# The state's part of the attention numerators as four 32-column products, the second state sum ahead of them, and the state layouts earlier on VectorE

## What is computed

```python
qkv = x @ wqkv                                   # 256 -> 768, 16 heads of 16 channels
q, k = relu(q), relu(k)
kv  = cumsum(k[..., :, None] * v[..., None, :], axis=2)
num = einsum('bhnd,bhnde->bhne', q, kv)
den = einsum('bhnd,bhnd->bhn', q, cumsum(k, axis=2))[..., None] + 1e-5
attention = (num / den).reshape(b, n, d) @ wo

scores = sigmoid(x @ Wr)                         # router, 8 experts, the best 2 are taken
hid = silu(x @ Wg[e]) * (x @ Wu[e])              # 4 experts with a hidden width of 128
ffn = sum_e cw[e] * (hid[e] @ Wd[e]) + (cw[4] + cw[6]) * x + cw[7] * relu(x) + conv4(x) + conv_b
```

## Time and profile before

| | before |
|---|---|
| median of 3 runs | 1421.67 us (1413.32 to 1422.32) |
| the profiled execution's own time | 1417.17 us |
| its span, first to last instruction | 1415.4 us |
| granted TensorE clock, mean | 0.994 of full speed |
| TensorE matmuls (PE) busy | 1373.6 us, 97% |
| TensorE weight loads (PEld) busy | 1194.5 us, 84% |
| VectorE (DVE) busy | 1087.9 us, 77% |
| GpSimd (POOL) busy | 811.6 us, 57% |
| ScalarE (ACT) busy | 734.5 us, 52% |

### The profile page before, as it was taken

One profiled execution on the slowest core, in us unless ns is written; L12 is line 12 of the kernel. 1 busy time (PEld: TensorE's weight loads), 2 busy tenths in 40 slices (PEclk: granted clock), 3 DMA queues, 4 the chain that ended last, 5 costly groups with the idle time before them and its releaser, 6 DMA issues.

```text
span 1415.4 us, 55195 instructions
## 1 busy us (share of the span) xinstructions
PE 1373.6 (97%) x23392; PEld 1194.5 (84%) x23392; DVE 1087.9 (77%) x2566; ACT 734.5 (52%) x1545; POOL 811.6 (57%) x679
## 2 busy tenths in 40 slices
PE   4999999999999999999999999999999999999997
PEld 3788887888888888888888888888888888878886
DVE  5778787778787778877777877788877788867874
ACT  5455554455554455554555554455544555535551
POOL 1755665655656655656556657556556556565553
PEclk9899999999999999999999999999999999999998
DMA  5011101111111121011111011111111111101110
GB/s 168 4 63 62 62 33 33 62 62 62 47 48 32 62 62 63 32 38 56 62 63 59 35 38 56 63 62 47 47 32 63 62 62 43 51 32 47 47 47 16
DMA packets 46790, 73.86 MB, mean 52 GB/s; under 512 B 6480, under 2 KB 42192, under 8 KB 42448
## 3 DMA queue, kind: packets, MB, share of 16 engines
q1 hardware_dynamic: 46544, 70.24, 14.7%
HBM read 53.18 MB, written 17.04 MB: 50 GB/s over the span
## 4 chain that ended last, share of the span: by engine, by line
PE 95%; DVE 2%; issue 1%; SPq 1%; ACT 1%; DMA 0%; DVEq 0%; ACTq 0%
PE ring L311 48%; PE scores L311 16%; PE ring L432 9%; PE ring L422 6%; PE scores L368 5%; PE state_sum L383 4%; PE scores L321 2%; PE ring L450 2%; PE scores L350 2%; DVE sm L764 1%; DMA x_t<-in_L_attn_x_dram 0%; DVE x_t L836 0%; SPq L268 0%; DVE cT L786 0%; ACT qp L527 0%
## 5 line engine op out<-in xcount | busy, mean ns | idle before, releaser
L637 POOL TENSOR_TENSOR hid<-hid,cwb 128x512 f32<-128x512 f32 x128 | 163.1, 1275 | 217.4 <-DVE hid L794 214.6
L786 DVE SCALAR_TENSOR_TENSOR cT<-xT,conv_ws,cT 128x512 f32<-128x512 f32 x192 | 256.9, 1377 | 0.0
L625 POOL TENSOR_TENSOR x_t<-x_t,same 128x1024 f32<-128x1024 f32 x32 | 76.9, 2404 | 286.3 <-ACT same L534 286.3
L550 ACT ACTIVATE sg<-ring 128x512 f32<-128x512 f32 x128 | 76.7, 599 | 303.1 <-PE ring L311 303.1
L311 PE MATMUL ring<-xl,wgu_h 128*128 128x512 f32 x512 | 212.9, 416 | 8.7 <-DVE x_t L836 6.8
L311 PE MATMUL ring<-xh,wgu_l 128*128 128x512 f32 x512 | 203.5, 397 | 0.0
L311 PE MATMUL ring<-xh,wgu_h 128*128 128x512 f32 x512 | 202.6, 396 | 0.0
L490 ACT ACTIVATE yh<-yT 128x256 fp32r<-128x256 f32 x128 | 53.6, 418 | 286.7 <-DVE yT L807 286.7
L794 DVE TENSOR_TENSOR hid<-ring,sg 128x512 f32<-128x512 f32 x128 | 88.2, 689 | 137.4 <-PE ring L311 137.2
L641 POOL TENSOR_TENSOR hl<-hid,hh 128x512 fp32r<-128x512 f32 x128 | 193.0, 1508 | 0.0
L764 DVE TENSOR_TENSOR sm<-scores,causal_s 128x512 f32<-128x512 f32 x256 | 159.0, 684 | 29.1 <-PE scores L368 28.6
(11 more groups left out here) (110 smaller groups left out, 3591.1 us busy)
## 6 DMA issues: line engine op xcount, KB each, us to landing
cwb<-cw_rows SPq DMA_DIRECT2D x32, 1024.0 KB, 4.8
x_t<-in_L_attn_x_dram SPq DMA_DIRECT2D x32, 512.0 KB, 5.2
out_dram<-x_t SPq DMA_DIRECT2D x32, 512.0 KB, 3.0
cw_rows<-cwt SPq DMA_DIRECT2D x128, 2.0 KB, 1.4
sm<-in_L_attn_wqkv_dram SPq DMA_DIRECT2D x2, 384.0 KB, 4.9
sm<-in_L_ffn_Wg_dram SPq DMA_DIRECT2D x2, 256.0 KB, 4.7
sm<-in_L_ffn_Wu_dram SPq DMA_DIRECT2D x2, 256.0 KB, 5.4
cwb<-in_L_ffn_Wd_dram SPq DMA_DIRECT2D x1, 512.0 KB, 5.6
```

The lines of the kernel that those rows point to most:

```text
L550: act.activation(sg[:, :], GB[t % 2], ACT.Silu).then_inc(s_sg, 1)
L625: pool.tensor_tensor(xb, xb, same[:, :, :], ALU.add).then_inc(s_base1, 1)
L637: pool.tensor_tensor(hid[:, e, :], hid[:, e, :], cwb[:, e, :], ALU.mult).then_inc(s_hid, 1)
L786: ins = dve.scalar_tensor_tensor(out=cT[:, c, :], in0=xT[:, j % 2, c, n:n + BT], scalar=conv_ws[:, c, n:n + 1], in1=cT[:, c, :], op0=ALU.m ...
```

## The change

The products with the state are cut by columns: in place of one matmul with 128 stationary columns there are four (m = 0 to 3) with 32 columns each, which write 32 partitions of the result each. All four read the same 64 columns of q on all 128 rows. The wait on s_bd for both chunks of the tile stands once, ahead of them. `state_sum(2t + 2)` moves from behind these products to ahead of them, right behind the products within the chunks. On VectorE `blocks(2t + 2)` moves ahead of `gate_up(t)` and `blocks(2t + 3)` ahead of the wait on s_num; before, both stood in `attend`, the second behind the product into `yT`.

```diff
@@ numerators (TensorE)
+                    if t < T - 1:
+                        state_sum(s, j, 0, 2 * t + 2)
+                    pe.wait_ge(s_bd, chunk_at(s, j, 2 * t + 1))
                     for h in range(2):
                         if first_tile and h == 0:
                             continue
-                        n = 2 * t + h
-                        pe.wait_ge(s_bd, chunk_at(s, j, n))
+                        n0 = t * P + h * HALF
                         for g in range(C):
-                            n0 = t * P + h * HALF
-                            ins = mm(NB2[t % 2][h][:, g * HALF:(g + 1) * HALF], state_bd[:, n % 4, g * P:(g + 1) * P],
-                                     qT[:, g, n0:n0 + HALF], start=False, stop=True, skip_group_check=True)
+                            for m in range(PPG):
+                                cols = slice(g * P + BLK * m, g * P + BLK * m + BLK)
+                                ins = mm(NB2[t % 2][h][BLK * m:BLK * m + BLK, g * HALF:(g + 1) * HALF],
+                                         state_bd[:, (2 * t + h) % 4, cols], qT[:, g, n0:n0 + HALF], start=False,
+                                         stop=True, skip_group_check=True)
                     ins.then_inc(s_num, 1)
-                    if t < T - 1:
-                        state_sum(s, j, 0, 2 * t + 2)
@@ attend and the loop over tiles (VectorE)
                 def attend(t):
-                    if t < T - 1:
-                        blocks(s, j, 0, 2 * t + 2)
-                    elif j < BPS - 1:
-                        blocks(s, j, 1, 0)
                     dve.wait_ge(s_num, at(s, j, T, t + 1))
...
+                for t in range(T):
+                    if t < T - 1:
+                        blocks(s, j, 0, 2 * t + 2)
+                    elif j < BPS - 1:
+                        blocks(s, j, 1, 0)
+                    gate_up(t)
                     if t < T - 1:
                         blocks(s, j, 0, 2 * t + 3)
-
-                for t in range(T):
-                    gate_up(t)
                     attend(t)
```

## The result

The changed kernel takes 1504.53 us in the median of 4 runs (1494.96 to 1506.51), the kernel before 1418.29 us (4 runs): 1.060 times as long, 95% interval 1.053 to 1.066. Faster was forecast; it is slower by 6%.

What follows compares the result with a forecast made beforehand. TensorE's sequence was taken as the bound. Savings of 37.8 us (88 full tiles), 1.9 (8 first tiles) and 7.4 (32 tiles t = 3), together 47 us from 1417.2, gave 1370, named 1371 us; range 1344 to 1398 us.

Steps and rivals of the forecast that it cites:

- What bounds the kernel: TensorE's own sequence, busy 97% of the span; time taken out counts in full while VectorE keeps up.
- The price p: Distance between starts of the new 128-row, 32-column records at line 435: 0.017 us, low end 0.010, high end 0.029.
- the two rivals with a higher price: Weight loads one at a time, 0.029 us, 1416 us (9%); column tiles on same rows not overlapping, 0.031 us, 1615 us (6%).
- the second of them: Line 435: column tiles on the same rows don't overlap, each record pays its tile's whole turn; 198 us lost, 1615 us (6%).
- The stretch of a tile: TensorE from the last record of line 422 to `gate_up`: 1.44 us before, 0.94 after, plus 0.07 for the wait.
- The wait of the second sum: `state_sum(2t + 2)` at line 383 waits for `blocks(2t + 2)` to read the bank it overwrites: 0.07 us a tile.
- the saved switch: Shape switch from line 432 to 383, up to 0.22 us; moved, the sum follows line 422 in the same shape at 0.02.
- VectorE: Keeps up, level with TensorE in t = 3; the rival that `blocks(2t + 2)` starts late gives 1396 us (12%).
- No transfer and no other queue is moved: Statement that the change leaves transfers and other queues alone; no term of the sum stands for them.

Runs made afterwards that it cites:

- e1_order: The changed kernel with the four old 128-column products per tile, so only the new order of sums and layouts: 1410.68 us against 1420.56, ratio 0.994.
- g1_cols64_pad40: The changed kernel with two 64-column products in place of four 32-column ones, and 40 tiny matmuls ahead of the loop: 1379.02 us against 1421.05, ratio 0.971.
- g2_cols64_pad44: The changed kernel with two 64-column products in place of four 32-column ones, and 44 tiny matmuls ahead of the loop: 1402.76 us, ratio 0.988.

## Why the prediction was wrong

**What bounds the kernel** held: TensorE's own sequence set the time before, and sets it now.

**The price p** was near: 0.017 us was taken and 0.014 measured, though no trace had shown the shape. Tiles over all 128 rows overlap, and the two rivals with a higher price (0.029 us, and over 0.031) fall with it. The kernel did end slower, as the second of them had it, but not by its mechanism. The two rules of the Trainium skill that stood beside those rivals, the floor of about 25 ns between starts and loads that overlap only where the row group differs, find no support in the 0.014 us.

**The stretch of a tile** came out at 1.05 us, where 0.94 and 0.07 for the wait were forecast. The wait of the second sum was mis-sized: line 383 starts 0.20 us behind the last record of line 422 in that tile, so it waits some 0.18 us; over the tiles without a stall it starts 0.09 to 0.20 us behind. The lower p makes up for it, and the stretch to `gate_up` is 0.96 to 1.04 us in the 16 such tiles. The order's own worth, which the sum has at 0.22 for the saved switch less 0.02 and 0.07, in 96 tiles 12 us, is 10 us in `e1_order`.

**VectorE** kept up: in `g1_cols64_pad40`, 42 us faster than before, it is 81% busy and no wait of TensorE for `state_bd` shows.

**The step that failed** is the one without a term. The prediction counts the added records, 24 in a full tile, at what they cost in the array, and says "No transfer and no other queue is moved". But TensorE's instructions are themselves a transfer: 24 more packets of 16.4 KB, and, what matters, 128 records in a row from line 383 to line 435, started within about 1.7 us (746.61 to 747.84 for the first 96, and 0.43 for line 435 where it isn't stopped). Where the grid cuts the program so that such a row fills a block, the block runs in 1.6 to 2.4 us, and the next one takes longer to come: its packet starts 0.8 to 1.4 us behind the block's start, takes about 1.0 us, and the engine goes on some 1.4 us behind its end, 3.5 us in all by the middle values. A late block cost 0.7 to 2.6 us from start to start, one or two blocks behind it came late too, and the idle time took the clock to half in places. 36 us of work were saved; 99 us of idle time and 26 us of clock were lost. The 64-column form at a lucky address comes within 8 us of the forecast of 1371 us: 1379 us. The 32-column form that was forecast was never seen without stalls.

The trace of the kernel before had a hint. Four of its issue waits lie in the last sequence, which stands behind the loop at other places of the grid. Three are at records 20764, 20890 and 21015, 126 and 125 apart, the first behind a block of 2.3 us; the fourth is at 21522, behind 125 records in 2.8 us. All four end 1.2 to 1.4 us behind a packet of the instruction queue. I took the 1% "issue" of the chain as nothing to explain.

**What stays open.** The packets' times answer in part why blocks behind a late one are late too, although they ran for 4.4 to 7.2 us. In the changed kernel, where one late block follows another, the packet starts only 3.8 to 6.8 us behind the restart, when the block that runs has nearly ended, in place of 0.8 to 1.4 us; a series ends where it comes early again (1.1 us behind the restart at record 1954). Why it starts late is not shown. The block of 2.2 to 2.4 us that ends at record 951 and brings no stall has no packet in it: in the sequence read, the packet ahead of it had started 2.8 us before the block began (642.74 against 645.5 us), so the next block was there. And in `g2_cols64_pad44` the block of 3.8 us had its packet only 2.0 us behind its start. So the bound isn't the block's length alone but when its packet starts, and what sets that start is open. That the block is late because it is being fetched is read from the grid, the shifts and the packets' ends; the profile itself names no releaser.

## What to carry to other kernels

Count instructions, not only array time: where a change splits a matmul into short ones, look at how long some 125 load-and-matmul records in a row take, and expect stalls of about 2 us, and in places the half clock behind them, where that is under 3 to 4 us. Stalls that name no releaser, fall between two records of one line and come back at the same record of each iteration are such stalls; a few tiny matmuls ahead of the loop move them, and are the cheapest test. The instruction queue's packets in the trace are the other one: here the stalls ended about 1.4 us behind one. And a kernel's time, before or after a change, can hang on such a shift by 6% (1419 us with 5 tiny matmuls, 1511 us with 27), so a change that adds or removes TensorE instructions should be judged at more than one.

## What the runs showed of the hardware

- Four column tiles over all 128 rows overlap: 32-column float32 records that move 64 columns start 0.014 us apart; two 64-column tiles need (0.69 - 0.23) / 15 = 0.031 us a record, so the same work in half the records takes nearly the same time (0.46 against 0.43 us).
- The waits for instructions are mostly 0.9 to 2.6 us from start to start and stand at fixed records, on a grid of 256 instructions or 124 to 126 records; each ended 1.2 to 1.9 us behind a packet of the instruction queue. A loop's jump cost 1.6 to 3.0 us in every kernel, and ended 1.5 to 1.7 us behind such a packet.
- Behind the idle stretch from 748.2 to 750.2 us the granted clock was 0.50 until 753.6; such falls came 20 times in the changed kernel and 4 times before, over the span 34.6 us of lost clock against 8.5 us.
